# Two buffers for the scan's states, four decays and residual sums on TensorE in a Mamba and SwiGLU layer

## The reference, cut to what matters

```python
h = rmsnorm(x) * norm_w
xs, res = split(h @ in_w.T)                      # 256 channels each
u = silu(causal_conv4(xs) + conv_b)
delta, B, C = split(u @ xp_w.T)                  # 64, 16, 16
delta = softplus(delta @ dt_w.T + dt_b)
state_t = exp(delta * A) * state_(t-1) + delta * u * B    # 256 channels x 16 states
y = (sum over 16 states of state_t * C + u * D) * silu(res)
x = layernorm(2 * x + y @ out_w.T)
x = layernorm(x + (silu(x @ wg.T) * (x @ wu.T)) @ wd.T)   # int weights times 1/127
```

## Time and profile before

| | |
|---|---|
| median of 3 runs (lowest to highest) | 610.42 us (609.94 to 611.24) |
| profiled execution: its time, its span | 610.23 us, 608.5 us |
| DVE busy | 534.5 us, 88% |
| PE, POOL, ACT busy | 425.8, 398.3, 355.9 us |
| DVE scans, 256 | 299.2 us |
| idle time of DVE before scans | 32.1 us |

### The profile page before, as it was taken

One profiled execution on the slowest core, in us unless ns is written; L12 is line 12 of the kernel. 1 busy time (PEld: TensorE's weight loads), 2 busy tenths in 40 slices (PEclk: granted clock), 3 DMA queues, 4 the chain that ended last, 5 costly groups with the idle time before them and its releaser, 6 DMA issues.

```text
span 608.5 us, 5732 instructions
## 1 busy us (share of the span) xinstructions
PE 425.8 (70%) x1477; PEld 172.9 (28%) x1477; DVE 534.5 (88%) x582; ACT 355.9 (58%) x594; POOL 398.3 (65%) x176
## 2 busy tenths in 40 slices
PE   4898586786598595887598695887597694467353
PEld 3332121322232241323232241322242241113142
DVE  4779997989998998989998999989998999999822
ACT  2675874496547675496547775497537774443221
POOL 5588597567776777576776688566776688575000
PEclk9988886997988987987988787987988787777756
DMA  8084044300660044400560043400660044400000
GB/s 213 2 180 98 0 89 95 93 1 1 137 152 5 1 99 80 114 0 0 138 151 4 0 97 93 103 0 0 138 155 0 0 99 92 103 1 0 17 1 18
DMA packets 27360, 39.11 MB, mean 64 GB/s; under 512 B 3816, under 2 KB 10056, under 8 KB 27344
## 3 DMA queue, kind: packets, MB, share of 16 engines
q1 hardware_dynamic: 25424, 38.51, 28.0%
q10 hardware_dynamic: 1920, 0.42, 0.4%
HBM read 3.27 MB, written 2.10 MB: 9 GB/s over the span
## 4 chain that ended last, share of the span: by engine, by line
DVE 37%; issue 22%; POOL 16%; PE 10%; ACT 7%; SPq 4%; DMA 3%; DVEq 1%; POOLq 0%; ACTq 0%
DVE state L904 19%; POOL prod L742 11%; DVE weighted L913 9%; SPq L326 4%; DMA du_rep<-z_wm 2%; PE dense_ps L449 2%; DVE g L920 1%; POOL rs L762 1%; ACT decay_ps L554 1%; DVE g_act L955 1%; PE dense_ps L447 1%; PE y_ps L427 1%; ACT L578 1%; ACT x L565 1%; DVE g_act L951 1%
## 5 line engine op out<-in xcount | busy, mean ns | idle before, releaser
L904 DVE TENSOR_TENSOR_SCAN state<-decay_ps,prod 128x512 f32<-128x512 f32 x256 | 299.2, 1208 | 32.1 <-ACT decay_ps L554 16.7
L742 POOL TENSOR_TENSOR prod<-du_rep,b_rep 128x2048 f32<-128x2048 f32 x63 | 284.8, 4530 | 41.5 <-DVE state L904 35.7
L554 ACT ACTIVATE decay_ps<-delta_rep,a_neg 128x512 f32<-128x512 f32 x252 | 169.8, 687 | 74.6 <-DVE state L904 74.2
L913 DVE TENSOR_TENSOR weighted<-state,c_ps 128x2048 f32<-128x2048 f32 x64 | 146.4, 2287 | 2.7 <-DVE state L904 0.6
L416 PE MATMUL c_ps<-xd,pick 96*128 96x512 f32 x128 | 84.4, 747 | 86.3 <-DVE weighted L913 86.3
L427 PE MATMUL y_ps<-weighted,gather 128*32 128x512 f32 x512 | 87.2, 760 | 6.4 <-DVE weighted L913 6.4
L762 POOL TENSOR_TENSOR rs<-ve,powm 128x4 f32<-128x4 f32 x16 | 16.2, 1012 | 104.5 <-ACT nm L560 104.5
L447 PE MATMUL dense_ps<-h_t,tap_t 128*128 128x512 f32 x128 | 58.9, 604 | 6.5 <-ACT h_t L599 6.5
L416 PEld LDWEIGHTS c_ps<-xd,pick 96*128 96x128 f32 x128 | 25.0, 222 | 120.0 <-DVE weighted L913 111.9
L559 ACT ACTIVATE ve<-mv 128x4 f32<-128x4 f32 x16 | 3.3, 206 | 71.4 <-DVE mv L939 44.1
L746 POOL TENSOR_TENSOR z_wm<-z_e,z_wm 128x512 f32<-128x512 f32 x15 | 18.7, 1269 | 30.3 <-ACT z_wm L622 25.3
(11 more groups left out here) (125 smaller groups left out, 550.0 us busy)
## 6 DMA issues: line engine op xcount, KB each, us to landing
du_rep<-z_wm SPq DMA_DIRECT2D x64, 256.0 KB, 5.0
delta_rep<-z_ln SPq DMA_DIRECT2D x64, 256.0 KB, 4.8
out_dram<-y_out SPq DMA_DIRECT2D x8, 256.0 KB, 4.6
state<-L_attn_in_proj_w_in ACTq DMA_DIRECT2D x1, 256.0 KB, 4.1
x_all<-L_attn_x_in SPq DMA_DIRECT2D x1, 256.0 KB, 4.5
weighted<-L_ffn_w_gate_in SPq DMA_DIRECT2D x1, 192.0 KB, 10.7
weighted<-L_ffn_w_up_in SPq DMA_DIRECT2D x1, 192.0 KB, 4.3
weighted<-L_ffn_w_down_in SPq DMA_DIRECT2D x1, 192.0 KB, 5.1
```

What stands on the lines that cost most here:

```text
L554: A(decay_ps[n % DECAYS][:, :], decay_ps[n % DECAYS][:, :] if spread_first else delta_rep[:, h, c, :], ACT.Exp, scale=a_neg[:, col:col + 1 ...
L742: TT(prod[quad % 2][:, :, :], du_rep[:, h, :, :], b, ALU.mult).then_inc(prod_ready, 1)
L904: dve.tensor_tensor_scan(state[:, n % BLOCKS, :], decay_ps[n % DECAYS][:, :], prod[n // BLOCKS % 2][:, n % BLOCKS, :], 0.0, ALU.mult, ALU. ...
L913: TT(weighted[quad % 2][:, :, :], state[:, :, :], c_ps[:, :].unsqueeze(1).broadcast_to([P, BLOCKS, T]), ALU.mult).then_inc(weighted_ready, 1)
```

## The change

- `state` has two buffers, by quad. `weigh` of quad q moves behind the first scan of quad q+1; that of quad 7 behind s0 of the next batch (behind s31 in the last scanned batch).
- The ring of decays has four places, the fourth, `decay_sb`, in SBUF.
- 2x is added by PE: four more matmuls (`twice` times x) end the proj job. ACT copies the sum to r1 at step 7; DVE's r1 instruction goes.
- x1 stays fp32 (`x1_t`): one fp32 matmul for each gate and up in the place of two fp32r ones; x1_lo goes.
- The two down jobs become one, with four more matmuls that add x1; the scale SILU2 goes into the weights; DVE's r2 goes, and `bn_stats` and the last normalisation read PSUM. b2 and b3 change banks.
- Steps move by one in many places: combine 2 to 3 and 18 to 19, first layernorm's statistics 6, 7 to 7, 8, their scale on ACT 8 to 10 and on POOL one quad later, SiLUs 10 to 11, tanh to 19, 20, 21, gates on DVE by one, z_ln 22 to 23.
- In the first batch POOL makes delta and du of the second half behind prod2 and no longer ahead of prod1; late weight copies on ACT are one step later.

```diff
-    DECAYS = 3
+    DECAYS = 4
...
-        state = sb("state", [P, BLOCKS, T])
+        state = pair("state", [P, BLOCKS, T])
...
-        decay_ps = [pb(f"decay_ps{i}") for i in range(DECAYS)]
+        decay_ps = [pb(f"decay_ps{i}") for i in range(DECAYS - 1)]
+        decay = decay_ps + [sb("decay_sb", [P, T])]
...
-                            last = mm(ps[:, i * P:(i + 1) * P], g[:, h, i * P:(i + 1) * P],
-                                      out_t[:, h, :], start=(h == 0), stop=(h == HALVES - 1))
+                            mm(ps[:, i * P:(i + 1) * P], g[:, h, i * P:(i + 1) * P], out_t[:, h, :],
+                               start=(h == 0), stop=False)
+                        at = (it.k0 - 1 + it.ahead) * TILES + i
+                        xk = x_all[:, at, :] if isinstance(at, int) else x_all[:, bass.ds(at, 1), :]
+                        last = mm(ps[:, i * P:(i + 1) * P], twice[:, :], xk, start=False, stop=True)
...
-                    w = (gate_t if kind == "gate" else up_t)[:, n, :]
-                    mm(ps[:, :], w, x1_hi[:, :], start=True, stop=False)
-                    last = mm(ps[:, :], w, x1_lo[:, :], start=False, stop=True)
+                    last = mm(ps[:, :], (gate_t if kind == "gate" else up_t)[:, n, :], x1_t[:, :], start=True, stop=True)
...
-                            last = mm(ps[:, i * P:(i + 1) * P], g_act[:, b, (2 * n + i) * P:(2 * n + i + 1) * P],
-                                      down_t[:, b, :], start=(b == 0), stop=(b == HID - 1))
+                            mm(ps[:, i * P:(i + 1) * P], g_act[:, b, i * P:(i + 1) * P], down_t[:, b, :],
+                               start=(b == 0), stop=False)
+                        last = mm(ps[:, i * P:(i + 1) * P], ident[:, :], x1[:, i, :], start=False, stop=True)
...
-                A(decay_ps[n % DECAYS][:, :], decay_ps[n % DECAYS][:, :] if spread_first else delta_rep[:, h, c, :],
+                A(decay[n % DECAYS][:, :], decay_ps[n % 3][:, :] if spread_first else delta_rep[:, h, c, :],
...
-                    if step == 10:
+                    if step == 11:
...
-                    if step == 13:
+                    if step == 14:
...
-                    if step == 22:
+                    if step == 23:
...
-                    for q, at in enumerate((23, 24, 27, 28)):
+                    for q, at in enumerate((24, 25, 27, 28)):
...
-                    if step == 8:
+                    if step == 7:
+                        it.wait_full(act, "proj")
+                        it.take(A(r1[:, :, :], it.ps("proj")[:, :].rearrange("p (i m) -> p i m", m=M), ACT.Copy), "proj")
+                    if step == 10:
...
-                        A(x1_hi[:, :], it.ps("x1")[:, :], ACT.Copy).then_inc(x1_hi_ready, 1)
-                    for b, at in enumerate((18, 19, 21)):
+                        it.take(A(x1_t[:, :], it.ps("x1")[:, :], ACT.Copy), "x1")
+                    for b, at in enumerate((19, 20, 21)):
...
-                        normalise(it, y_out[it.next], r2, rs2, nmr2, shift2_ready, y_ready)
+                        ps = it.ps("down")
+                        it.take(normalise(it, y_out[it.next], lambda i: ps[:, i * P:(i + 1) * P], rs2, nmr2,
+                                          shift2_ready), "down")
...
-                    soften(it, 1)
-                    scale_u(it, 1)
...
-                    if it.outs and quad == 2:
+                        if it.k0 == 0 and quad == 2:
+                            soften(Iteration(-1), 1)
+                            scale_u(Iteration(-1), 1)
+                    if it.outs and quad == 3:
...
-                for n, (dst, ps) in enumerate(((down_t, decay_ps[1]), (up_t, decay_ps[2]))):
-                    dve.wait_ge(wt_turned, 6 + n)
-                    dve.tensor_copy(dst[:, :, :].rearrange("p b h -> p (b h)"), ps[:, 0:HID * P]
-                                    ).then_inc(wt_taken, 1)
+                dve.wait_ge(wt_turned, 6)
+                TS(down_t[:, :, :].rearrange("p b h -> p (b h)"), decay_ps[1][:, 0:HID * P], SILU2, None, ALU.mult
+                   ).then_inc(wt_taken, 1)
+                dve.wait_ge(wt_turned, 7)
+                dve.tensor_copy(up_t[:, :, :].rearrange("p b h -> p (b h)"), decay_ps[2][:, 0:HID * P]
+                                ).then_inc(wt_taken, 1)
...
-                it.wait(dve, weighted_ready, QUADS, 0, n // BLOCKS)
+                if n % BLOCKS == 0:
+                    it.wait(dve, weighted_ready, QUADS, 0, n // BLOCKS - 1)
...
-                dve.tensor_tensor_scan(state[:, n % BLOCKS, :], decay_ps[n % DECAYS][:, :],
+                dve.tensor_tensor_scan(state[n // BLOCKS % 2][:, n % BLOCKS, :], decay[n % DECAYS][:, :],
...
-            def weigh(it, quad):
-
-                it.wait(dve, scanned, GROUPS, 0, BLOCKS * (quad + 1))
-                it.wait(dve, summed, QUADS, 0, quad - 1)
-                it.wait(dve, c_ready, QUADS, 0, quad + 1)
-                TT(weighted[quad % 2][:, :, :], state[:, :, :],
+            def weigh(it, quad, batch=0):
+
+                it.wait(dve, scanned, GROUPS, batch, BLOCKS * (quad + 1))
+                it.wait(dve, summed, QUADS, batch, quad - 1)
+                it.wait(dve, c_ready, QUADS, batch, quad + 1)
+                TT(weighted[quad % 2][:, :, :], state[quad % 2][:, :, :],
...
-                    if step == 2:
+                    if step == 3:
...
-                    if step == 6:
-                        it.wait_full(dve, "proj")
-                        lo = (it.k0 - 1 + it.ahead) * TILES
-                        xk = x_all[:, lo:lo + TILES, :] if isinstance(lo, int) else x_all[:, bass.ds(lo, TILES), :]
-                        it.take(STT(out=r1[:, :, :], in0=xk, scalar=2.0,
-                                    in1=it.ps("proj")[:, :].rearrange("p (i m) -> p i m", m=M),
-                                    op0=ALU.mult, op1=ALU.add), "proj")
+                    if step == 7:
...
-                    if step == 7:
+                    if step == 8:
...
-                    if step == 16:
-                        it.wait(dve, x1_hi_ready, 1, -1, 1)
-                        it.take(TT(x1_lo[:, :], it.ps("x1")[:, :], x1_hi[:, :].bitcast(f32), ALU.subtract), "x1")
-                if it.scan and step == 18:
+                if it.scan and step == 19:
...
-                    for b, (at, then) in enumerate(((19, 20), (20, 21), (22, 23))):
+                    for b, (at, then) in enumerate(((20, 21), (21, 22), (23, 24))):
...
-                    for b, (at, then) in enumerate(((19, 20), (20, 21), (22, 23))):
+                    for b, (at, then) in enumerate(((20, 21), (21, 22), (23, 24))):
...
-                    if step in (26, 27):
-                        n = step - 26
-                        it.wait_full(dve, f"down{n}")
-                        it.take(STT(out=r2[:, 2 * n:2 * n + 2, :],
-                                    in0=it.ps(f"down{n}")[:, 0:2 * M].rearrange("p (i m) -> p i m", m=M),
-                                    scalar=SILU2, in1=x1[:, 2 * n:2 * n + 2, :],
-                                    op0=ALU.mult, op1=ALU.add), f"down{n}")
...
-                    if it.outs and n in (7, 28):
-
-                        it.wait(dve, ln1_step if n == 7 else ln2_step, 1, -1, 1)
...
-                        if n % BLOCKS == BLOCKS - 1:
-                            weigh(it, n // BLOCKS)
+                    if it.outs and n in (8, 28):
+                        it.wait(dve, ln1_step if n == 8 else ln2_step, 1, -1, 1)
+                    if it.scan:
+                        if n % BLOCKS == 0 and n > 0:
+                            weigh(it, n // BLOCKS - 1)
+                        elif n == 0 and it.outs:
+                            weigh(it, QUADS - 1, -1)
...
+                if it.k0 == B - 1:
+                    weigh(it, QUADS - 1)
```

More of the change, by code:

```diff
@@ L67, in mamba_swiglu_postln @@
         out_t = sb("out_t", [P, HALVES, M])
-        gate_t = sb("gate_t", [M, HID, P], f32r)
-        up_t = sb("up_t", [M, HID, P], f32r)
+        gate_t = sb("gate_t", [M, HID, P])
+        up_t = sb("up_t", [M, HID, P])
         down_t = sb("down_t", [P, HID, M])
@@ L81, in mamba_swiglu_postln @@
         ident = sb("ident", [P, P])
+        twice = sb("twice", [P, P])
         pick = sb("pick", [XC, 2 * CHUNKS, P])
@@ L119, in room @@
             return cut
-        cut = room(state[:, :, :])
+        cut = room(state[0][:, :, :])
         in_raw = cut(P, 2 * HALVES * M).rearrange("p (c m) -> p c m", m=M)
@@ L143, in mamba_swiglu_postln @@
         x1 = sb("x1", [P, TILES, M])
-        x1_hi = sb("x1_hi", [M, T], f32r)
-        x1_lo = sb("x1_lo", [M, T], f32r)
+        x1_t = sb("x1_t", [M, T])
         g_th = sb("g_th", [P, 2, T])
         g_act = sb("g_act", [P, HID, T])
-        r2 = sb("r2", [P, TILES, M])
         st2 = sb("st2", [P, TILES, 6])
@@ L237, in mamba_swiglu_postln @@
                 ["C", "S", "up2", "b0", "b1"],
```

(43 more changed lines are left out.)

9 lines of the change are left out of this document (3 added, 6 removed).

## The result

The changed kernel takes 652.53 us in the median of 4 runs (649.59 to 654.5) against 610.18: 1.0687 times the time before, 95% interval 1.0644 to 1.0729. Slower was forecast, but at 631.5 us in a range of 616 to 641, so half of the loss was missed. The profiled execution took 652.44 us, its span is 650.7.

A forecast was written before the change was run, and what follows sets the result against it. A loop through DVE, ACT, POOL and DMAs was taken to bound each 68.24 us batch, not DVE's work. 610.23 - 0.6 (first batch) + 18.6 (six batches at +3.1) + 1.2 + 2.1 (end) = 631.5 us, range 616 to 641.

The forecast's parts named there:

- part B: Loop stretch from tt0 over gate2, tanh, z_ln, delta, the DMAs and prod0 to the next s0: 25.51 us, forecast +0.6.
- What I take at nothing: SBUF decays in eight scans a batch and bn_stats from PSUM: 0.2 us a batch at most, taken as 0.
- tt0: Start of DVE's g_act product that frees gate2's bank, where the loop is cut: 42.73 us behind s0.
- part A: DVE's stretch of the loop from s0 to tt0: 42.73 us, forecast +2.5 us.
- The start of the batch: In part A, PE's cold c_ps waits for late w7, so h_t, exp4 and s4 come late: +2.2 us.
- Ends: First batch -0.6 us (s16 near 67.8), last scanned batch +1.2, everything behind the last scan +2.1.
- the cold start: PE's lower clock at the batch start; the 2.2 us would shrink to 0.3 if PE were warm.
- PE warm: Rival: PE warm at the batch start, or h_t's path otherwise short; batch +1.2, 620 us; chance 0.17.
- the last scanned batch and the tail: Last batch: instructions and own waits go, w7 and waits come, +1.2; behind the last scan proj and down grow, +2.1.
- one more exp ahead of z_ln: In part B, one more exp before z_ln's table load on ACT: +0.6 us.
- more than that: Rival: more PE idling puts down at the lower clock, a batch takes 2.2 us more: 645 us; chance 0.13.
- Faster: Rival: DVE is the bound and the loop gives way: 577 us, or 594 with half of it; chance 0.08.

The follow-up runs named there:

- a_ps3: The changed kernel without its fourth decay, so three decays, all in PSUM: 647.98 us, 1.0622 times the kernel before.
- ps3_w7: a_ps3 with only w7, the last weigh of a batch, put back ahead of the next s0: 618.58 us.
- after_first: The changed kernel with POOL's first-batch order as before (delta and du of the second half ahead of the products): 650.72 us.
- after_warm: The whole change plus seven products with unread results on PE ahead of c_ps: 634.3 us.
- best6: The kernel before with two state buffers, residual sums on PE and six added PE products with unread results, POOL's first-batch order kept: 596.6 us, ratio 0.9763.

## Why the prediction was wrong

Against 631.5 the profiled execution took 20.9 us more. It divides, by the table, into the first batch 6.8 (s0 at 106.46, forecast 99.6), six batches 13.3 (73.70, forecast 68.38 + 3.1), and what lies behind the last s0 0.7 (102.0, forecast 98.0 + 1.2 + 2.1).

- **The step that failed in part B: "What I take at nothing".** Eight scans a batch from SBUF were priced by two products of DVE, 0.692 and 0.67 us, without a look at what POOL did beside them. As an operand the SBUF decay did cost nothing: 1203 ns in the median, 1204 from PSUM. But B was forecast at 26.3 by the table's mean (25.72 + 0.6) and took 27.5 in each of the six batches: 7 us in all, of which a_ps3 gives back 3 to 4. In the batch read, s0 comes 5.52 us behind prod0's start where 4.56 had passed before: that is the hold of s31. prod0 itself comes 22.0 behind tt0 (forecast 21.6), behind POOL's reciprocal root, which waited for the aggregation that s27's hold had made late; the forecast had the DMAs last there by 0.9 us, though the earlier trace rows shows prod0 without a wait for a DMA. The row that speaks against the step stood in the earlier trace rows: a POOL product of 1.77 where such products take 1.27; I used its end and passed over its length. The Trainium skill (SBUF: SBUF — State Buffer, sections "SBUF: two separate sides" and "Who interferes with whom") says that a DVE instruction with two SBUF inputs and a GpSimd instruction that reads SBUF exclude each other, and that the one that "starts first gets the pair for the whole instruction; the other fully blocks". This case's traces agree: 4.67 and 5.42 us for 1.20, and 2.18 for 1.27 on the other side. I had looked up what an operand costs and not who shares its port.
- **The step that failed in part A: "The start of the batch".** The mechanism was right as far as it went. s4 waited 1.71 us, the combine 0.70, c_ps and y_ps ran at 0.50. Missing was that the lower level lasts through xs0: 5.3 to 5.75 us for 3.70 in four of six batches, so that r1 comes late for the statistics (1.75, a wait that the forecast said would not be). A is 46.5 to 47.1 there and 44.7 in the two batches where xs0 took 3.70; the forecast was 45.2. That is 1.0 a batch, 6 us. The move of w7 was priced at 2.2 + 2.2 = 4.4 in A, and ps3_w7 measures 4.3, but in both of its kernels xs0 was slow in some batches, so the agreement is in part luck.
- **"Ends", the first batch.** du of the second half was put at 50.5. In the trace prod2 waited 1.22 for DVE, which s3's hold of 4 us had made late, delta was held (2.07 for 1.27), and du ended at 55.4; s16 came at 72.42, not 67.8. The other 2.2 us lie in its second half, with late weighs and the holds of s27 and s31. How these share them was not tested: a_ps3, without holds, has the second batch's s0 0.9 us earlier, after_first 3.1.
- **What weighs most.** Not the SBUF decay: a_ps3 leaves it out and still takes 16 us more than forecast. The first batch and PE's lower level are what remain there. after_warm brings the whole change to 634.3, inside the range, but of its 18.2 us the forecast had counted some 11 as the cold start (2.2 - 0.3, six times); for a kernel with PE warm it said 620. So that nearness is no confirmation.
- **Right:** the last scanned batch and the tail (+4.0, forecast +3.3), one more exp ahead of z_ln (z_ln reached POOL 6.12 behind tt0, before 5.61), a wait of 3 to 5 us at s0 in a_ps3 (3.2 to 4.7), s14's wait. s13's wait of 1 us was not there. DVE's busy time, forecast to fall by 17 us, rose by 34.8, as the profile books the holds as busy; without them, in a_ps3, it fell by 21.5.
- **The rival "more than that"** came nearer (645), but by the wrong place: down ran at the upper level and hid behind s27's hold.
- **"Faster"** was right on what part of the edits can give: best6 gets 14 of its 16 us (594), by part A and not by part B, as B stays at 25.9.

Why removing one loss gave so little: in a_ps3 the gate2 product of the loop falls to the lower clock, and z_ln reaches POOL 7.07 us behind tt0 instead of 6.12, which takes back half of what the holds had cost: B is 26.8 in that batch, against 27.5 in the changed kernel and 26.1 as forecast:

```profile
372.33 2.08 PE L475 MATMUL dense_ps<-x_t,gate_t 128*128 128x512 f32 x2
```

In the changed kernel it took 1.13. That it did so because PE had idled longer there is the reading of one batch's row (3.31 us idle ahead of up1, before gate2), not a test.

## What to carry to other kernels

Before you move an operand to SBUF, ask which engine shares the port at that moment, not only what the operand costs: a scan went from 1.2 to 5.4 us, and the profile booked it as busy time. An engine that only fills gaps still sets the pace if its clock falls in them and something waits for it: then a few idle products were worth nearly 2% (608.4 to 597.4 us), and nothing where nobody waited (610.5). Test the parts of a bundle alone: here one was worth 2% with the right company, others cost 7%, and the sum showed neither.
